# A fused transformer-block kernel without the seven products on zeros at the head of TensorE's program

## The reference

```
x = x + windowed_attention(layernorm(x))     # 16 heads of 8, 2 key/value heads, windows of 64 keys per 32 queries
x = x + ffn(layernorm(x))
x = x + linear_attention(layernorm(x))       # elu + 1 features, normalised
x = x + ffn(layernorm(x))                    # the same weights again
```

## Time and profile before

| | |
|---|---|
| median of 3 runs | 565.35 us (562.87 to 565.62) |
| the profiled execution | 563.48 us |
| its span, first to last instruction | 561.5 us |
| mean granted TensorE clock | 0.991 |
| PE busy | 525.0 us, 93% of the span, 5070 records |
| DVE busy | 439.8 us, 78% |
| POOL busy | 453.3 us, 81% |
| ACT busy | 359.9 us, 64% |
| the removed line, L876 | 14 records, 9.3 us |

### The profile page before, as it was taken

One profiled execution on the slowest core, in us unless ns is written; L12 is line 12 of the kernel. 1 busy time (PEld: TensorE's weight loads), 2 busy tenths in 40 slices (PEclk: granted clock), 3 DMA queues, 4 the chain that ended last, 5 costly groups with the idle time before them and its releaser, 6 DMA issues.

```text
span 561.5 us, 14744 instructions
## 1 busy us (share of the span) xinstructions
PE 525.0 (93%) x5070; PEld 343.3 (61%) x5070; DVE 439.8 (78%) x1264; ACT 359.9 (64%) x578; POOL 453.3 (81%) x654
## 2 busy tenths in 40 slices
PE   5876898979999999999999999999999999999886
PEld 2542554546766667667667675666666666677654
DVE  2879899998988888888888888888888888663430
ACT  1543375667677677776777767767777677755632
POOL 8337698989999989899898989898989788955640
PEclk9997999999999999999999999999999999999998
DMA  9433332322222322232322222232222221200011
GB/s 307 133 86 90 73 75 68 85 68 68 54 59 58 81 60 79 62 82 67 83 63 72 68 67 52 66 80 58 77 64 65 67 58 39 58 1 20 1 28 29
DMA packets 49546, 38.88 MB, mean 69 GB/s; under 512 B 12352, under 2 KB 38976, under 8 KB 49472
## 3 DMA queue, kind: packets, MB, share of 16 engines
q1 hardware_dynamic: 47024, 33.73, 24.0%
q10 hardware_dynamic: 2448, 4.22, 2.1%
HBM read 15.64 MB, written 5.51 MB: 38 GB/s over the span
## 4 chain that ended last, share of the span: by engine, by line
PE 79%; DVE 10%; issue 3%; POOL 3%; DMA 2%; ACT 1%; DVEq 0%; SPq 0%; POOLq 0%; ACTq 0%
PE ring L589 18%; PE ring L601 17%; PE ps_s L557 9%; PE ring L531 8%; PE ps_o L574 5%; PE ring L612 5%; PE ring L632 4%; PE ring L682 2%; PE ring L659 2%; PE ring L621 2%; DVE merged L1194 2%; DMA out_x<-x_G 2%; PE ring L876 2%; DVE ps_o L1208 1%; DVE rowmax L1188 1%
## 5 line engine op out<-in xcount | busy, mean ns | idle before, releaser
L476 POOL TENSOR_TENSOR probs_t<-probs_t,first 128x1024 f32<-128x1024 f32 x64 | 151.5, 2369 | 7.6 <-DMA probs_t<-probs_t 7.6
L601 PE MATMUL ring<-w,early 128*128 128x128 f32 x1024 | 120.0, 275 | 1.9 <-DVE x_L L1166 1.0
L601 PEld LDWEIGHTS ring<-w,early 128*128 128x128 f32 x1024 | 117.9, 192 | 4.5 <-issue 2.0
L918 ACT ACTIVATE early<-ring,b 128x512 f32<-128x512 f32 x128 | 86.9, 681 | 36.3 <-PE ring L589 34.4
L908 ACT ACT_TABLE_LOAD x58 | 74.4, 1283 | 10.3 <-issue 9.3
L927 ACT ACTIVATE probs_t<-merged_t 128x1024 f32<-128x1024 f32 x64 | 67.0, 1049 | 20.0 <-DVE merged_t L1201 18.0
L557 PE MATMUL ps_s<-kx,q_t 64*32 64x512 f32 x960 | 65.7, 604 | 8.2 <-DVE merged L1194 7.2
L589 PE MATMUL ring<-xT_G,w1b 128*128 128x512 f32 x128 | 65.1, 617 | 0.7 <-ACT xT_G L896 0.7
L589 PE MATMUL ring<-xT_F,w1b 128*128 128x512 f32 x128 | 59.2, 605 | 0.4 <-ACT xT_F L896 0.4
L1208 DVE STREAM_TRANSPOSE ps_o<-ps_o 128x512 f32<-128x512 f32 x64 | 46.0, 719 | 11.0 <-PE ps_o L574 10.9
L1181 DVE COPY_PREDICATED ps_s<-first,ps_s 128x512 f32<-128x512 uint32 x64 | 43.9, 687 | 13.6 <-PE ps_s L557 13.2
(11 more groups left out here) (122 smaller groups left out, 1023.6 us busy)
## 6 DMA issues: line engine op xcount, KB each, us to landing
probs_t<-probs_t SPq DMA_DIRECT2D x256, 64.0 KB, 2.0
kx<-kv_rows SPq DMA_DIRECT2D x120, 40.0 KB, 2.2
x_P<-in_x SPq DMA_DIRECT2D x16, 256.0 KB, 3.2
out_x<-x_G SPq DMA_DIRECT2D x16, 256.0 KB, 3.2
vx_t<-kv_rows SPq DMA_DIRECT2D x128, 8.0 KB
up_s<-in_up_m ACTq DMA_DIRECT2D x7, 256.0 KB, 7.6
down_s<-in_down_m ACTq DMA_DIRECT2D x7, 256.0 KB, 7.7
kv_rows<-kv_t SPq DMA_DIRECT2D x16, 80.0 KB, 2.8
```

What stands on the lines that cost most here:

```text
L476: nc.gpsimd.tensor_tensor(parts, parts, keep.rearrange("p (a t) -> p a t", a=1).to_broadcast([P, PAIR * HEADS, WIN]), ALU.mult).then_inc(p ...
L601: last = nc.tensor.matmul(bank(name)[:, P * j:P * (j + 1)], hid[s][:, c, P * j:P * (j + 1)], w2[:, c], start=(c == 0), stop=(c == CH - 1))
L918: nc.scalar.activation(hid[s][:, c], bank(name)[:], ACT.Gelu, bias=b1[:, c:c + 1]).then_inc(drained[BANK[name]].sem, 1)
```

## The change

The seven products go, with the two semaphores and with the memset of d_tmp that fed them. TensorE still waits for `first_in` at its head. The order of everything else is the same on each engine.

```diff
--- before.py
+++ after.py
@@ -244,8 +244,6 @@
         vones_in = sem("vones_in")
         u_in = sem("u_in")
         d_in = sem("d_in")
-        zeroed = sem("zeroed")
-        warmed = sem("warmed")
         up_in = [sem(f"up_in{n}") for n in range(INNER)]
         down_in = [sem(f"down_in{n}") for n in range(INNER)]
         half_set = sem("half_set")
@@ -871,10 +869,6 @@
                     linear_state(g)
 
             pe.wait_ge(first_in, 16)
-            pe.wait_ge(zeroed, 1)
-            for n in range(7):
-                last = nc.tensor.matmul(ring[3][:], d_tmp[:, 0], d_tmp[:].rearrange("p c n -> p (c n)"), start=True, stop=True)
-            last.then_inc(warmed, 1)
             for t in range(TURNS):
                 turn(t)
 
@@ -1251,7 +1245,6 @@
                 if i == 0:
                     dve.wait_ge(outer_in, 16)
                     dve.wait_ge(d_in, 16)
-                    dve.wait_ge(warmed, 1)
                 dve.wait_ge(down_outer, 2 * CH * i)
                 outer_stage(nc.vector, lambda c: d_t[i][:, c], d_t[1 - i], d_tmp, down_cs, 1 - i, down_outer, 2 * CH * i)
 
@@ -1384,7 +1377,6 @@
                 for g in due(t, 0):
                     moments(g, "P")
 
-            nc.vector.memset(d_tmp[:], 0.0).then_inc(zeroed, 1)
             for t in range(TURNS):
                 turn(t)
```

## The result

The changed kernel took 561.09 us in the median of five runs (560.93 to 562.82) against 565.35 (562.87 to 565.62, five runs): ratio 0.9948, 95% interval 0.9924 to 0.9972. It is faster, by about 2.9 us; forecast were 2.4. Timed once more beside the experiments (12 runs, 35 of before), it came out at 0.9977 (0.9953 to 1.0001): 1.3 us, and the interval just reaches no change. So the gain is small, and its size is known only to lie somewhere between 1 and 3 us. The forecast's ratio, 0.9957, lies inside both intervals. The profiled execution took 560.95 us against 563.48: 2.5 us less.

The account below looks back on a forecast made before the run. A fill of some 60 us with no engine full, then a body bound by TensorE. Lead 4.74 us less 2.3 for the slow clock leaves 2.4, taking the median from 565.35 to 562.9 us; range 559.7 to 566.4.

Parts of the forecast that it names:

- Data: Start of the head: the first real product has its data and can start at about 8.2 us, against 14.4 before.
- ScalarE: Head: free at 10.75 us to drain the first half stage; up_stage(1, "b") starts at 11.24, not 15.98, lead 4.74 us.
- VectorE: Head: outer stages start at 10.3 us, not 15.2, a lead of 4.9, and are no longer waited for by TensorE.
- The clock: Head from 11.24 us: real work runs at 1.2 GHz until a rise at 16.5, costing 2.3 us and leaving 2.4.
- One sign: TensorE's first matmuls, at 8.1 to 8.7 us: weight loads of about 0.34 us each would show the slow clock.
- Passage to the end: From the first scores of group 0 onward: the lead of about 2.4 us arrives with nothing lost.
- Early rise: Rival at the head: the clock rises early or its slow part is cheap; saving 4.2 us, time 561.1; chance 0.09.
- Absorbed: Rival in the fill: something else paces it and the body starts when it did; about 565 us; chance 0.15.
- Slower by the clock in the thin part of the fill: Rival at 21 to 50 us: low clock slows seven score groups, 0.87 us each; 569.1 with middle lead; chance 0.13.

Follow-up runs that it names:

- up_diag late: The changed kernel with GpSimd's four up_diag products moved from its first turn to the end of its second; ratio 0.9968 to the kernel before.
- changed + five: The changed kernel with five products on constants put into TensorE's waits of the fill; ratio 0.9922 to the kernel before, median 559.33 us.
- idle head: The changed kernel with TensorE and VectorE's outer stage held until the fifth stage matrix is in, at about 14.2 us; ratio 1.0049 to the kernel before.
- the five products: Five products on constants in TensorE's waits before scores of groups 0 and 1; added to the kernel before with its seven kept, ratio 0.9969.

## Why the prediction was right

Step by step, in the forecast's own order:

1. *Data.* Start at 8.2: it was 8.17.
2. *ScalarE.* Free at 10.75, next half stage at 11.24: 10.76 (the first drain) and 11.22. Lead 4.74 forecast, 4.76 measured.
3. *VectorE.* "The outer stages then start at 10.3 ... a lead of 4.9": they started at 10.21, but this step was wrong beyond the start. They ended at 16.7, a lead of 2.6, since the first ran beside GpSimd's up_diag and took 3.27 us instead of 0.87. In the first profile this was hidden by 0.47 us (the wait at 17.20 for P.kv); in the second it wasn't, and cost some 0.4 us (22.07 against the 21.66 of up_diag late). The Trainium skill has the rule ("SBUF — State Buffer", Who interferes with whom): a tensor_scalar can take the port pair that VectorE shares with GpSimd, and then one blocks the other for the whole instruction. The trace agrees: 3.27 us beside GpSimd, 0.87 without. In the kernel before, the zeros held VectorE's outer stage back until up_diag was done, so d_tmp shows no overlap there, and I had not asked what its earlier start would collide with. But the price was in that trace all the same, one step ahead, at xn_P, the same kind of instruction (four, 128x128 float32), which takes 1.86 us at 8.43 beside these two groups of GpSimd's and 1.11 where up_diag is late:

```profile
8.55 0.54 POOL L460 TENSOR_TENSOR up_mix<-outer 128x8 f32<-128x8 f32 x2
9.17 4.03 POOL L465 TENSOR_TENSOR up_diag<-first,up_mix 128x512 f32<-128x512 f32 x4
```

4. *The clock.* Rise at 16.5, price 2.3 us, X.kb between 18.2 and 19.4: loads were slow at 15.01 and fast at 16.96, and the lead went from 4.76 to 2.48, a price of 2.28. X.kb ended at 18.69. That it came out to a tenth is luck: in the second profile of the same kernel the rise came sooner, the price was 1.17 and X.kb ended at 17.42, outside the 18.2 to 19.4 (17.36 in up_diag late and 17.76 in changed + five). The mechanism is right, and the size was taken from two instances where executions differ by more than 1 us. One sign was off: the loads of the first products took 0.22 us each (1.79 us for eight) and not 0.34; at full clock such loads take 0.13 (0.52 for four). The Trainium skill ("TensorE: Matmul & The Clock Gate", What's actually happening) has the throttled state as the default which activity releases; idle head agrees, with 1.06 against 0.60 us for the same transposes.
5. *Passage to the end.* Priced at nothing lost. The first profile bears it out: 2.78 at the end of the head, 2.60 at the end of the fill, 2.54 at the last residual. The second doesn't: 3.40, 1.26, 1.10. So the price of nothing holds in an execution whose clock falls as it does in the kernel before, and not in every one.

The steps were right in kind. That the total came so near is in part luck: the lead at the head was larger than 2.4 (2.78 and 3.40), and in one of two profiles most of it was lost on the way. The forecast of 562.9 stood on the shown median; the measured median was 1.8 lower. Of that 0.5 is the ratio (0.9948 x 565.35 = 562.4), and the rest is that the shown median was high for this kernel: the mean of the same five runs is 564.6, and over 94 runs on four chips, timed with the experiments, the medians of the kernel before were 563.3 to 564.3.

*The rivals.* Early rise: it occurs, and then VectorE caps it at 22.08. Absorbed: not in the first profile, where 2.54 us are left at the end; in the second the clock's falls in other places took 2.30 of 3.40, as that rival had it, and the second ratio's interval reaches 1. Slower by the clock in the thin part of the fill: the mechanism is real and common, but it is there with and without the seven products. Over the timed runs of one group the mean granted clock was 0.9872 in the changed kernel and 0.9879 in the kernel before, so the two pay about the same. Whether the change adds a little is open: a fall between 28 and 37 us is seen in three of the four profiles without products at the head or in the fill, and in one of the six with some at the head alone; that is too few to tell. What goes with the falls between 44 and 60 us are TensorE's waits for VectorE: with the five products in them the clock stayed at 1.00 from 20 to 70 us in all four such profiles. The five are worth about 0.003 on the kernel before (0.9969) and 0.003 to 0.0055 on the changed one (0.9922 against 0.9948 or 0.9977).

## What to carry to other kernels

Products on zeros ahead of real work pay only while the engine would wait anyway: seven from 5.7 us, which ran on beyond the landing of the first real data, cost 1.3 to 2.9 us net. In true waits of the fill they gained. At the head, in idle time, two or four of them brought X.kb forward by 1.1 to 2.5 us in the profiles, but no gain in time over none at all was shown. When a wait is taken from one engine, look at which other engine's work its next instruction will now run beside; the row of that instruction in the trace before cannot show the price, but another of its kind beside the same work may. To judge a change at the head, follow one event (here the first copy_predicated) and the same lead at two or three later events before believing or doubting the total, and in more than one profile: here the end of X.kb moved by 1.3 us between two of one kernel.

## What was not expected of the hardware

- VectorE's copies from SBUF to SBUF (tensor_scalar, 128x128 float32, four of them) took 3.27 us beside GpSimd's tensor_tensor and 0.87 without. The same kind of instruction writing keys from PSUM kept its 3.94 to 3.98 us for eight in all kernels, with GpSimd's normalisation running beside it. GpSimd's up_diag took 4.03 us in both cases.
- The granted clock fell in places that differ from execution to execution of one program (28 to 34, 44 to 60, 118 to 130, 545 to 552 us), never from 160 to 500 us, where TensorE is all but full. TensorE need not be idle for long: around the falls of the fill its longest waits were 1.9 to 2.5 us, and between 118 and 130 us it was busy for 9.87 us of 12. A fill without any such fall took 129.4 and 130.3 us, with one or two 130.9 to 132.7, with three 133.2 to 136.0. This and the store's waits go with much of the scatter of 5 to 6 us between runs of one kernel. Over the 35 runs of before timed with the second group, the six with a mean clock of 0.991 had a mean of 562.0 us, the nine with 0.985 one of 565.5.
- A store of 256 KB landed 5.5 us after its issue in one turn, and in 3.2 us in the median; what delays it wasn't looked into.
